# An early tile of each expert ahead of the last chunk's scatter, in a Mamba and mixture-of-experts layer

## The reference

```python
x = layernorm(x + mamba(x))          # D_INNER 256, 16 states, scan over 1024 tokens
logits = xf @ w_g                    # 2048 tokens, 8 experts
topv, topi = top_k(logits, 2)
probs = softmax(logits kept at topi) # the others -1e9
capacity = 640                       # per expert: int(2 * 1.25 * 2048 / 8)
rank = cumsum(one_hot(topi))         # first choices of all tokens, then second
exp_batches = the kept rows of each expert, at its slots
h = gelu(exp_batches @ c_fc)         # 128 -> 512
exp_out = h @ c_proj                 # 512 -> 128
out = sum over a token's choices of probs * exp_out
x = layernorm(x + out)
```

## Time and profile before

| | |
|---|---|
| three runs | 379.01, 379.59, 379.95 us; median 379.59 |
| profiled execution, its own time | 379.31 us |
| its span, first to last instruction | 377.6 us |
| mean granted TensorE clock | 0.921 |
| TensorE products, busy | 289.0 us, 77% |
| VectorE, ScalarE, GpSimd busy | 283.8, 220.5, 264.7 us |

### The profile page before, as it was taken

How to read it: one execution, slowest core, us unless ns; L and a number is a source line. 1 busy time by engine, 2 the same in 40 slices (tenths; PEclk the granted TensorE clock), 3 DMA queues, 4 the chain that set the end, 5 groups by cost and what they waited for, 6 DMA issues and landing times. The chain is left out here.

```text
span 377.6 us, 5742 instructions
## 1 busy us (share of the span) xinstructions
PE 289.0 (77%) x1795; PEld 221.6 (59%) x1795; DVE 283.8 (75%) x448; ACT 220.5 (58%) x450; POOL 264.7 (70%) x224
## 2 busy tenths in 40 slices
PE   8797899677877739967564899775089999999900
PEld 6445456455765425757452564333089999999900
DVE  2699889999999799999889899996213444444655
ACT  1858987969965695776767665852203333333405
POOL 4607589977898799978989997896623555555532
PEclk9999999999999997968986799999589999999965
DMA  7061078564354254212112231001151434435773
GB/s 225 17 226 57 2 216 270 183 168 158 85 174 131 92 155 146 91 63 99 69 58 78 92 112 56 0 15 42 36 147 38 132 110 119 119 90 155 212 193 112
DMA packets 35693, 42.87 MB, mean 114 GB/s; under 512 B 3830, under 2 KB 26235, under 8 KB 35664
## 3 DMA queue, kind: packets, MB, share of 16 engines
q1 hardware_dynamic: 32240, 37.32, 32.4%
q0 software_dynamic: 2304, 4.24, 3.4%
q10 hardware_dynamic: 1120, 0.97, 0.8%
HBM read 30.11 MB, written 12.79 MB: 114 GB/s over the span
## 5 line engine op out<-in xcount | busy, mean ns | idle before, releaser
L1451 POOL TENSOR_TENSOR product<-state,c_wide 128x1024 f32<-128x1024 f32 x64 | 149.9, 2346 | 38.1 <-DVE state L1690 25.4
L1073 ACT ACTIVATE psum<-dt,a_neg 128x512 f32<-128x512 f32 x86 | 57.6, 684 | 32.6 <-DVE state L1690 31.2
L689 PE MATMUL psum<-ident,product 128*128 128x128 f32 x384 | 53.3, 285 | 17.4 <-POOL product L1451 17.4
L1690 DVE TENSOR_TENSOR_SCAN state<-psum,drive 128x512 f32<-128x512 f32 x50 | 59.7, 1212 | 4.3 <-ACT psum L1073 4.1
L689 PEld LDWEIGHTS psum<-ident,product 128*128 128x128 f32 x384 | 45.4, 147 | 27.6 <-POOL product L1451 24.0
L1661 DVE TENSOR_TENSOR drive<-dtu,psum 128x1024 f32<-128x1024 f32 x45 | 54.0, 1200 | 3.6 <-PE psum L656 3.6
L1575 POOL DMA_INDIRECT result_rows<-state,result_at x30 | 31.2, 1040 | 35.3 <-DVE state L1912 24.5
L1690 DVE TENSOR_TENSOR_SCAN state<-psum,carry,drive 128x512 f32<-128x512 f32 x40 | 50.4, 1270 | 0.2
L1912 DVE TENSOR_SCALAR state<-psum,result_weight 128x128 f32<-128x128 f32 x40 | 14.1, 351 | 38.9 <-PE psum L953 29.7
L940 PE MATMUL psum<-product,fc_sb 128*128 128x128 f32 x320 | 42.3, 275 | 1.1 <-DVE product L1872 1.1
L1532 POOL DMA_INDIRECT slot_rows<-sent,scatter_at x32 | 32.8, 1025 | 10.3 <-issue 6.8
(11 more groups left out here) (258 smaller groups left out, 541.2 us busy)
## 6 DMA issues: line engine op xcount, KB each, us to landing
c_wide<-c_rows SPq DMA_DIRECT2D x32, 512.0 KB, 4.1
slot_rows<-blank SPq DMA_DIRECT2D x8, 325.0 KB, 4.8
c_wide<-slot_rows SPq DMA_DIRECT2D x8, 325.0 KB, 3.7
result_rows<-zeros SPq DMA_DIRECT2D x8, 256.0 KB, 5.0
late_rows<-zeros SPq DMA_DIRECT2D x8, 256.0 KB
fc_sb<-in_c_fc SPq DMA_DIRECT2D x8, 256.0 KB
proj_sb<-in_c_proj SPq DMA_DIRECT2D x8, 256.0 KB
c_wide<-result_rows SPq DMA_DIRECT2D x8, 256.0 KB
```

Source lines behind the costliest of these rows:

```text
L689: last = nc.tensor.matmul(y_part(j, d), product[:, i, d, j * P:(j + 1) * P], ident[:, :], is_transpose=True, start=False, stop=True, skip_ ...
L1073: nc.scalar.activation(psum[:, A_BANK + d, :], dt[:, q % 2, d, :], ACT.Exp, scale=a_neg[:, n:n + 1]).then_inc(decay_ready, 1)
L1451: nc.gpsimd.tensor_tensor(product[:, U % PRODUCTS, channels, :], state[:, U % RING, channels, :], wide, ALU.mult).then_inc(product_ready, 1)
L1690: nc.vector.tensor_tensor_scan(state[:, U % RING, d, :], decay, rows, before, ALU.mult, ALU.add).then_inc(scanned, 1)
```

## The change

Each expert gets one early tile, made of slots that chunks 0 to 2 have filled: lane p of it is slot p (first tile, a first choice) where more than p first choices of the expert have been counted in chunks 0 to 2, and slot 512 + p (last tile, a second choice) elsewhere. After the last scan step TensorE counts the choices so far (one product with ones), and VectorE's `count_early` makes from it three masks per expert (`swap`) and moves the second choices of the last chunk down where fewer than 128 rows are there.

When chunk 2 has been scattered, SyncE loads the first and last tile of every expert (`load_early`, eight DMAs of 133 KB, two per pair of experts). By pairs VectorE masks them (`mask_early`), TensorE adds the two by transposes into the same PSUM place (`turn_early`), and VectorE copies them (`copy_early`) into `early_chan`. The first scatter of the last chunk now also waits until all eight early loads have landed (they read the table that it writes). TensorE goes through 40 tiles as before, tiles 0 to 7 the early ones, one per expert, then four late tiles per expert: the three middle ones and one in which the complementary parts of the first and the last are added the same way (`mask_rows`, `turn_rows`). The 26 warm-up products become 8 and start without waiting for a scatter. The weights of all eight experts stay in memory, in buffers that are free by then; those of experts 2 to 7 are loaded beside the scan of chunks 2 and 3, through the same SyncE queue as the C rows. VectorE centers all of them beside the early tiles, in the order of the last part of the diff. Hidden activations use a ring of four tiles. GpSimd scatters the early results behind the last chunk's scatters and ahead of the late results. Empty slots hold zeros, and the place in a row is written minus `NOWHERE`, which `tag_early` and `tag_results` add back.

```diff
-ROW_SETS = 4
+ROW_SETS = 3
+LATE_TILES = SLOT_TILES - 1
...
+        def weights_of(e):
+            homes = [first_weights[:, :, :, :].rearrange("p e k m -> p (e k m)"), x_tok[:, :, :].rearrange("p j m -> p (j m)"),
+                     z_tok[:, :, :].rearrange("p j m -> p (j m)"), u[:, 1, :]]
+            both = homes[e // 2][:, e % 2 * 2 * D_HID:(e % 2 + 1) * 2 * D_HID]
+            return both[:, 0:D_HID], both[:, D_HID:].rearrange("p (h m) -> p h m", h=HT)
...
+        early_chan = drive[:, 0, :, :].rearrange("p d t -> p (d t)")
+        rows_out = state[:, 0:2, :, :].rearrange("p a b (j d) -> p a (b j) d", d=D_MODEL)[:, :, 0:LATE_TILES, :]
+        early_out = drive[:, 1, :, :].rearrange("p d (j m) -> p (d j) m", m=D_MODEL)
...
+            def load_weights(e):
+                first, second = weights_of(e)
+                sp.dma_start(first, c_fc[bass.ds(e, 1), :, :].rearrange("e p m -> p (e m)")).then_inc(weights_loaded, 16)
+                sp.dma_start(second, c_proj[bass.ds(e, 1), :, :].rearrange("e (h p) m -> p (e h) m", p=P)).then_inc(weights_loaded, 16)
+            def load_early(g):
+                by_tile = slot_rows.rearrange("(e s p) d -> p e s d", s=SLOT_TILES, p=P)
+                for e in (2 * g, 2 * g + 1):
+                    sp.dma_start(early_rows[:, e, :, :], by_tile[:, e, 0:SLOT_TILES:LATE_TILES, :]).then_inc(early_loaded[g], 16)
...
+                    load_weights((m - 16) // 2)
+                if m in (20, 22):
+                    sp.wait_ge(x_turned, NQ)
+                    load_weights(2 + (m - 20) // 2)
+                if m in (29, 30):
+                    for part in "ab":
+                        bank, before = JOB[f"y2{part}"]
+                        sp.wait_ge(w_made[bank], before + 1)
+                    load_weights(4 + m - 29)
+                if m == 31:
+                    sp.wait_ge(dtu_ready, DT * NQ)
+                    sp.wait_ge(summed, DT * ((NQ - 1) * D_STATE + 1))
+                    load_weights(6)
+                    load_weights(7)
+            sp.wait_ge(seconds_sent, 16 * (TILES - TPC))
+            sp.wait_ge(firsts_sent, 16 * (TILES - TPC))
+            sp.wait_ge(product_ready, LAST + 1)
+            sp.wait_ge(last_product_ready, 1)
+            for g in range(PAIRS):
+                load_early(g)
             sp.wait_ge(seconds_sent, 16 * TILES)
             sp.wait_ge(firsts_sent, 16 * TILES)
             for e in range(ROW_SETS):
                 load_rows(e)
-            for e in range(2, N_EXP):
-                sp.wait_ge(fc_done, SLOT_TILES * (e - 1))
-                load_first(e // 2, e % 2)
-                if e + 2 < N_EXP:
-                    sp.wait_ge(rows_turned, e - 1)
-                    sp.wait_ge(tags_copied, e - 1)
-                    load_rows(e + 2)
-                sp.wait_ge(proj_done, SLOT_TILES * (e - 1))
-                load_second(e // 2, e % 2)
+            for e in range(ROW_SETS, N_EXP):
+                sp.wait_ge(rows_turned, e - ROW_SETS + 1)
+                sp.wait_ge(tags_copied, 2 * (e - ROW_SETS + 1))
+                load_rows(e)
...
+            pe.wait_ge(marks_carried, NQ - 1)
+            nc.tensor.matmul(psum[:, B_BANK + 1, 0:TOP_K * N_EXP], ones[:, :], marks[:, 0:TOP_K, :, 0], start=True, stop=True).then_inc(early_counted, 1)
...
+            def turn_early(g):
+                pe.wait_ge(early_masked, g + 1)
+                if g >= 2:
+                    pe.wait_ge(early_chan_ready, g - 1)
+                for i in range(2):
+                    to = psum[:, g % 2, i * P:(i + 1) * P]
+                    nc.tensor.matmul(to, early_rows[:, 2 * g + i, 0, 0:D_MODEL], ident[:, :], is_transpose=True, start=(i == 0), stop=True,
+                                     skip_group_check=True)
+                    last = nc.tensor.matmul(to, early_rows[:, 2 * g + i, 1, 0:D_MODEL], ident[:, :], is_transpose=True, start=False, stop=True,
+                                            skip_group_check=True)
+                last.then_inc(early_turned, 1)
             def turn_rows(e):
                 pe.wait_ge(rows_loaded[e % ROW_SETS], 16 * (e // ROW_SETS + 1))
-                if e:
-                    pe.wait_ge(rows_chan_ready, e)
-                for s in range(SLOT_TILES):
-                    last = nc.tensor.transpose(psum[:, s // TPC, (s % TPC) * P:(s % TPC + 1) * P], rows_in[:, e % ROW_SETS, s, 0:D_MODEL], ident[:, :])
-                last.then_inc(rows_turned, 1)
+                pe.wait_ge(rows_masked, e + 1)
+                if e >= 2:
+                    pe.wait_ge(rows_chan_ready, e - 1)
+                def turn(at, s, first):
+                    return nc.tensor.matmul(psum[:, e % 2, at * P:(at + 1) * P], rows_in[:, e % ROW_SETS, s, 0:D_MODEL], ident[:, :],
+                                            is_transpose=True, start=first, stop=True, skip_group_check=True)
+                for at in range(LATE_TILES):
+                    turn(at, at + 1, at == 0)
+                turn(LATE_TILES - 1, 0, False).then_inc(rows_turned, 1)
...
-            pe.wait_ge(seconds_sent, 16 * (TILES - TPC))
-            pe.wait_ge(firsts_sent, 16 * TILES)
-            for _ in range(26):
+            pe.wait_ge(weights_loaded, 16 * 2 * N_EXP)
+            for _ in range(8):
                 nc.tensor.matmul(psum[:, 2, 0:P], ident[:, :], ident[:, :], start=True, stop=True)
-            turn_rows(0)
-            first_product(0, 0)
-            turn_rows(1)
-            for e in range(N_EXP):
-                for s in range(SLOT_TILES):
-                    if s + 1 < SLOT_TILES:
-                        first_product(e, s + 1)
-                    elif e + 1 < N_EXP:
-                        first_product(e + 1, 0)
-                    second_product(e, s)
-                if e + 2 < N_EXP:
-                    turn_rows(e + 2)
+            turn_early(0)
+            turn_early(1)
+            first_product(0)
+            for k in range(FFN_TILES):
+                if k + 1 < FFN_TILES:
+                    first_product(k + 1)
+                if k in (0, 2):
+                    turn_early(2 + k // 2)
+                if k == N_EXP - 2:
+                    turn_rows(0)
+                second_product(k)
+                if k == N_EXP - 1:
+                    turn_rows(1)
+                if k >= N_EXP:
+                    e, s = divmod(k - N_EXP, LATE_TILES)
+                    if s == LATE_TILES - 1 and e + 2 < N_EXP:
+                        turn_rows(e + 2)
...
+                    if q == NQ - 1:
+                        gp.wait_ge(firsts_sent, 16 * TPC * q)
+                        for g in range(PAIRS):
+                            gp.wait_ge(early_loaded[g], 32)
...
+            gp.wait_ge(early_tagged, 4)
+            for e in range(N_EXP):
+                gp.wait_ge(rows_out_ready, e + 1)
+                to, bound = (result_rows, RESULTS) if e < N_EXP - 2 else (late_rows, 2 * TOKENS)
+                gp.indirect_dma_start(out=to, out_offset=bass.IndirectOffsetOnAxis(ap=early_at[:, e:e + 1], axis=0),
+                                      in_=early_out[:, e, :], in_offset=None, bounds_check=bound - 1, oob_is_err=False).then_inc(early_sent, 16)
...
+            def count_early():
+                dve.wait_ge(early_counted, 1)
+                dve.wait_ge(minus_half_made, 2)
+                firsts, seconds = (psum[:, B_BANK + 1, k * N_EXP:(k + 1) * N_EXP] for k in range(TOP_K))
+                nc.vector.tensor_copy(missing[:, :], firsts).then_inc(dve_step, 1)
+                for t, op in enumerate((ALU.is_gt, ALU.is_le, ALU.is_gt)):
+                    nc.vector.tensor_scalar(swap[:, :, t], firsts, own_lane[:, 0:1], None, op).then_inc(dve_step, 1)
+                dve.wait_ge(dve_step, step.up(4))
+                chain(nc.vector.tensor_tensor(missing[:, :], missing[:, :], seconds, ALU.add))
+                chain(nc.vector.tensor_scalar(missing[:, :], missing[:, :], -1.0, float(P), ALU.mult, ALU.add))
+                chain(nc.vector.scalar_tensor_tensor(marks[0:1, 1, :, 0], missing[0:1, :], 0.0, marks[0:1, 1, :, 0], ALU.max, ALU.add))
...
+            def mask_early(g):
+                pair = slice(2 * g, 2 * g + 2)
+                dve.wait_ge(early_loaded[g], 32)
+                part = early_rows[:, pair, :, :]
+                nc.vector.tensor_tensor(part, part, swap[:, pair, 0:2].unsqueeze(3).to_broadcast([P, 2, 2, ROW]),
+                                        ALU.mult).then_inc(early_masked, 1)
+            def copy_early(g):
+                dve.wait_ge(early_turned, g + 1)
+                nc.vector.tensor_copy(early_chan[:, 2 * g * P:2 * (g + 1) * P], psum[:, g % 2, 0:2 * P]).then_inc(early_chan_ready, 1)
...
+            def take_early(e):
+                dve.wait_ge(proj_done, e + 1)
+                nc.vector.tensor_scalar(early_out[:, e, :], proj_tile(e), early_tags[:, e, 1:2], None, ALU.mult).then_inc(rows_out_ready, 1)
+            def mask_rows(e):
```

(35 more changed lines are left out.)

185 lines of the change are left out of this document (105 added, 80 removed).

## The result

The changed kernel takes 381.62 us (median of 13 runs, 379.17 to 382.78) where the kernel before takes 379.59 (13 runs beside them, 378.49 to 380.68): a ratio of 1.0046, 95% interval 1.0028 to 1.0063. It is slower: the difference is small, 0.5%, but the whole interval lies above 1. Predicted were 372.1 us and a range of 369.0 to 376.0. The profiled execution took 381.71, with a span of 379.8.

The account below looks back on a forecast made before the run. TensorE was taken to bound the expert stage. The span was T 289.2 + late part 61.9 + tail 19.0, 370.1 us, 7.5 less than 377.6; execution 371.8, median 372.1 us, range 369.0 to 376.0.

Parts of the forecast that it names:

- What bounds the kernel, and the room: Expert stage: TensorE-bound, 80 products and 7 turns, 75.3 us; before it TensorE idle 261.9 to 273.1, room the change uses.
- T: Start of the first late product (first product 8): forecast 289.2; span equal to the kernel before at 296.7.
- The early loads and the scatters they hold back: Last chunk's scatters wait for eight early loads, move by 4.2 us, land at 282.1; expert 0's rows at 285.2.
- The early tiles, T = 289.2: Early stage: VectorE's instruction prices, added up from 265.42, put the first late product at 289.2.
- VectorE's queue, not the data, sets T: End of the early stage: VectorE's instruction order sets T at 289.2; with data as the limit, 287.1.
- Rival A: Early stage data-bound rather than VectorE-bound: T 286.1 to 287.5, time 369.0 to 370.4 us; chance 0.13.
- The clock: TensorE in the early stage: starts at 1.2 instead of 2.4 GHz, full clock by 275 to 277 once densely fed.
- Rival B: Half clock through the early stage: T 297.1, 2.0 us slower, 381.6 us; chance 0.06.
- Rival C: Clock falls once more, ahead of turn_rows(0) or between early tiles: 1.6 to 4 us back, 373.7 to 376; chance 0.13.
- The tail "keeps its order, so 19.0 stays": After the last product (take, scatter, landing, load, add, normalize, store): order kept, so 19.0 us stays.
- Edits costed at nothing: Count before the last chunk, weight loads in the scan, memset and iota at the start: covered, costed at nothing.
- The chances: Whole kernel: faster 0.89, same 0.03, slower 0.08; 370.4 to 374.4 us at 0.63.

Follow-up runs that it names:

- experiment 6: Changed kernel with the early results' scatters held until six early tiles are taken: 377.35 us, ratio 0.9961.
- experiment 1: Changed kernel with the last chunk's eight scatters held back until six early tiles are taken: 392.67 us, ratio 1.0348.
- experiment 2: Kernel before with 14 groups of four dummy matmuls, each followed by a GELU on ACT, ahead of the warm-up matmuls: 388.53 us.
- second kernel of 11: Changed kernel with early tiles of experts 6 and 7 multiplied ahead of these experts' late ones, and early results' scatters held until six early tiles taken: 389.77 us.
- 10: Changed kernel without the four loads of second-choice results (1 MB), VectorE adding the block's input instead: 378.66 us, ratio 0.9972.
- 11: Changed kernel with early tiles of experts 6 and 7 multiplied ahead of their late ones: 383.47 us; with results' scatters held 389.77; first version with VectorE's order mended 381.63.
- 7: Changed kernel again, unedited: 380.66 us (one run); the kernel with early results' scatters held, again: 377.20 us, ratio 0.9920.
- 5: Changed kernel with dummy matmuls between the sixth early first product and fifth early second product: 30 of them 384.18 us, 14 of them 377.42 us.

## Why the prediction was wrong, step by step

- **What bounds the kernel, and the room**: right. The span is T + late part + tail, and the late part came out at 62.3 for 61.9.
- **The early loads and the scatters they hold back**: right, 1.9 us mis-sized. First pair landed by 267.68 (predicted 267.4), first scatter at 272.43 (270.6), rows' load issued at 284.10 (282.1). The eight issues took 4.92 us instead of 4.2, and the first scatter started 1.15 us after the last early load had landed (271.28), a step that I had at nothing. By the data alone, with the 3.07 from issue to mask and the 2.10 from mask to T of experiment 6, the first trace would have had 284.10 + 5.17 = 289.3, as forecast.
- **The early tiles, T = 289.2**: the step that failed, +6.3 us. I summed the prices of instructions and took each handover between engines at its usual 0.02 to 0.1 us. Beside scatters issued back to back the updates of TensorE came up to 7.4 us late in three of four traces of this kernel. In the first that is 5.3 us of idle TensorE, and the fall of the clock behind it: four products in 287.62 to 294.20, 6.6 us instead of 3.6, so 3.0 more. Against that stands slack, since the first products were warm sooner than I had assumed. The size of the single terms is of one execution. That the lateness goes with the row of scatters is shown by experiments 1 and 2 and by the second kernel of 11, where it comes, goes and comes back with them. But it is not the only way to a late T: the one trace of this kernel without it had T = 294.4 and 380.66 us, by a late landing of the last scatter and the clock's fall.
- **VectorE's queue, not the data, sets T**: wrong even without late updates. In experiment 6 TensorE ran the stage at its own 1.79 us per tile, was done at 287, and waited for rows. Rival A had that limit but its T, 286.1 to 287.5, did not occur: without late updates and with eight scatters in a row it was 290.6 to 294.4.
- **The clock**: "full by 275 to 277" was near the truth in several traces (0.50 until 274.2 in experiment 1, 275.3 in 6 and 10); in the first one it was full from 270 on. Rival B did not happen; that its 381.6 us is the measured time is luck. Rival C, a fall at a stop between early tiles for 1.6 to 4 us, did, with 3.0; it was the consequence of the stop that I had no price for. The rule cited from the Trainium skill ("TensorE: Matmul & The Clock Gate", "HAM oscillation — how this bites in real kernels"), that waits between product bursts bring half rate back, agrees with the trace in this one place: 1.50 us idle left the clock at 1.00, 3.83 did not.
- **The tail "keeps its order, so 19.0 stays"**: the second step that failed, +2.9 us. The order stayed, the room didn't. The results of experts 0 to 5 are loaded beside the tiles of experts 6 and 7. These are now eight instead of ten, so the loads start 10.6 us ahead of the last product's end (347.24 to 357.8) instead of 14.1 (344.46 to 358.6). The 2 MB of them and the late loads then share the last microseconds with the last scatters. Experiments 10 and 11 show it.
- **Edits costed at nothing**: right. The chain reached the last chunk's routing 0.3 us earlier than before; the count and the weights' loads cost nothing that the trace shows.
- **The chances**: with a tail of 21.9 and a late part of 62.3 the break-even is T = 377.6 - 84.2 = 293.4, not 296.7. The 3.3 us that I believed to have as a margin weren't there, and "slower" had only 0.08.

Open: what decides whether the updates get stuck, which all traces of a group had in common, and whether executions that nobody recorded have it at all; whether it is the write into PSUM or the message that is late; why a landing took 4.0 us in the second trace of the changed kernel; and where the hold of experiment 6 gains. A hint on both: from the last scatter's start to the rows' load it took 4.00 and 3.57 us in the two traces without late updates in which the results' scatters follow the eight at once (experiments 7 and 5), and 2.30 and 2.61 in the two with the hold. Its two traces had no late update, but its other twelve executions, up to 380.5 us, have no trace.

## What to carry to other kernels

Work moved beside a stage that was quiet before meets that stage's traffic, and a chain that passes from engine to engine sixteen times feels it sixteen times: look in the trace for the same handshake beside the same traffic, and if there is none, measure it with a probe such as experiment 2 before counting on it. Take the trace of the unedited kernel again in each group of runs: an effect that is absent in the edited kernel may be absent in its neighbour too. Work taken out of the end of a kernel also takes the cover off what ran beside it there, so the tail has to be summed anew. And a bound that comes out equal to another one within its errors (VectorE 289.2, data 287.1) is no margin.
